# Both attentions of an audio tower: x normalised on VectorE and split into fp16 halves before the transposes

## The reference, cut to what matters

```python
h = _L0_tok_ref(x)                                   # 128 sequences of 32 tokens, 512 wide
h = h + _L0_attn_ref(_layernorm(h), wq, wk, wv, wo)  # 32 heads of 16, 8 for k and v, rotary, causal
h = h + _L0_ffn_ref(_layernorm(h), w1, w3, w2)       # ternary weights
h = h + _L1_attn_ref(_layernorm(h), Wq, Wk, Wv, Wo)  # 16 heads of 32, 4 for k and v, bias, causal
h = h + _L1_ffn_ref(_layernorm(h), gate_up, down)    # 4-bit weights
```

## Time and profile before

| | |
|---|---|
| runs | 2387.38, 2389.77, 2393.89 us |
| median | 2389.77 us |
| profiled execution | 2391.57 us |
| its span in the profile | 2389.8 us |
| mean granted clock of TensorE | 0.985 of full speed |
| busy, PE | 2244.2 us, 94% |
| busy, DVE | 1662.7 us, 70% |
| busy, ACT | 1495.3 us, 63% |
| busy, POOL | 1021.4 us, 43% |

### The profile page before, as it was taken

How to read it: one execution, slowest core, us unless ns; L and a number is a source line. 1 busy time by engine, 2 the same in 40 slices (tenths; PEclk the granted TensorE clock), 3 DMA queues, 4 the chain that set the end, 5 groups by cost and what they waited for, 6 DMA issues and landing times. The chain is left out here.

```text
span 2389.8 us, 41107 instructions
## 1 busy us (share of the span) xinstructions
PE 2244.2 (94%) x13188; PEld 1128.5 (47%) x13188; DVE 1662.7 (70%) x2931; ACT 1495.3 (63%) x2398; POOL 1021.4 (43%) x1007
## 2 busy tenths in 40 slices
PE   6999999998999996799999999999987999999998
PEld 2333333335666663344444445666652444444443
DVE  6666666665888887456667634666657888888873
ACT  4666666666788785355656425667745666667663
POOL 1222222237777773223324302444434555555552
PEclk9999999999999998799999999999999999999999
DMA  5545445442343211312223212222221011111101
GB/s 146 138 127 135 129 127 135 130 110 66 111 131 114 67 58 36 109 50 79 80 89 93 67 48 84 80 79 79 79 67 40 23 49 40 53 41 45 45 27 53
DMA packets 144300, 194.94 MB, mean 82 GB/s; under 512 B 32773, under 2 KB 76261, under 8 KB 144154
## 3 DMA queue, kind: packets, MB, share of 16 engines
q1 hardware_dynamic: 115642, 154.79, 21.7%
q10 hardware_dynamic: 28512, 38.28, 5.7%
HBM read 125.10 MB, written 42.21 MB: 70 GB/s over the span
## 5 line engine op out<-in xcount | busy, mean ns | idle before, releaser
L341 DVE TENSOR_REDUCE tm_negmax<-tm_s 128x1 f32<-128x512 f32 x512 | 323.3, 679 | 164.7 <-PE tm_s L384 164.4
L303 ACT ACTIVATE tm_prob<-tm_s 128x1024 f32<-128x1024 f32 x256 | 257.6, 1023 | 136.9 <-PE tm_s L404 130.6
L2119 PE MATMUL f_part<-f_xhi,gu 128*128 128x512 f16 x704 | 269.4, 383 | 17.8 <-ACT f_firstg L1922 6.3
L2119 PE MATMUL f_part<-f_xlo,gu 128*128 128x512 f16 x704 | 268.6, 382 | 0.0
L421 PE MATMUL tm_o<-tm_prob,tm_vt 128*64 128x512 f32 x1024 | 255.7, 620 | 0.0
L1888 POOL TENSOR_TENSOR f_firstg<-f_firstg,f_secondg 128x512 f32<-128x512 f32 x88 | 150.7, 1712 | 193.3 <-DVE f_secondg L2006 193.3
L2141 PE MATMUL f_pz<-dn,f_ghi 128*128 128x512 f16 x704 | 214.5, 380 | 5.9 <-ACT f_zc L1954 5.9
L384 PE MATMUL tm_s<-tm_qk 96*128 96x512 f16 x512 | 199.2, 391 | 14.6 <-DMA tm_qk<-tm_xs 14.1
L264 POOL TENSOR_TENSOR tm_hn<-tm_nd,tm_rows 128x1024 f32<-128x1024 f32 x32 | 75.3, 2353 | 291.8 <-DMA tm_rows<-rden 291.8
L404 PE MATMUL tm_s<-tm_qk 98*128 98x512 f16 x512 | 194.2, 382 | 1.6 <-DMA tm_qk<-tm_mrow 1.6
L975 PE MATMUL a_bankB<-a_wo,a_yThi 128*128 128x512 f16 x512 | 158.7, 393 | 4.1 <-DVE a_yTlo L899 4.0
(11 more groups left out here) (190 smaller groups left out, 5668.4 us busy)
## 6 DMA issues: line engine op xcount, KB each, us to landing
tm_qk<-tm_xs SPq DMA_DIRECT2D x384, 64.0 KB, 2.1
tm_xqk<-in_qk ACTq DMA_DIRECT2D x32, 512.0 KB, 4.3
a_hin<-h SPq DMA_DIRECT2D x64, 256.0 KB, 2.7
a_hres<-h SPq DMA_DIRECT2D x64, 256.0 KB, 3.0
h<-a_hout SPq DMA_DIRECT2D x64, 256.0 KB, 2.5
f_hin<-h SPq DMA_DIRECT2D x64, 256.0 KB, 2.7
f_hres<-h SPq DMA_DIRECT2D x64, 256.0 KB, 2.8
tm_vt<-in_vt ACTq DMA_DIRECT2D x32, 256.0 KB, 3.0
```

The costliest lines, as they stand in the source:

```text
L303: nc.scalar.activation(prob[b][:, 2 * h:2 * h + 2, :], s2[:, i % 2, :, :], ACT.Exp, scale=SCALE).then_inc(exp_done, 1)
L341: nc.vector.tensor_reduce(negmax[u][:, m:m + 1], s1[:, p % BANKS, :], AX.X, ALU.max, negate=True).then_inc(s1_read, 1)
L2119: last = nc.tensor.matmul(part[q % BANKS][:, :], (gate, up)[which][:, j, m * P:(m + 1) * P], xparts[x][u][:, j, :], start=x == 0, stop=x == 1)
```

## The change

In both attentions the normalised row is made by DVE, into one buffer (`xn` has been two). ACT casts it to the high half, and the low half is the difference, made by DVE in the first attention and by POOL in the second. Both halves lie in one buffer, `halves`, and are transposed by PE as eight fp16 blocks into bankA, which is read as 1024 fp16 columns. ACT copies both transposed halves at once into `xs` (two buffers). `offset` and the subtraction from the bank are gone. `project` reads the same operands as before from the new buffer.

```diff
-    veps, shift_by = pair("veps", [P, 1], F32), pair("shift_by", [P, 1], F32)
-    xn = pair("xn", [P, DM], F32)
-    xhi, xlo = pair("xhi", [P, KT, P], F16), pair("xlo", [P, KT, P], F16)
+    veps = pair("veps", [P, 1], F32)
+    xn, halves = sb("xn", [P, DM], F32), sb("halves", [P, 2, DM], F16)
+    xs = pair("xs", [P, 2, KT, P], F16)
...
 def gpsimd(pool):
...
+        def x_low(t):
+
+            if inside(t, TILES) and not rope:
+                wait_alone(pool, s["pool_passed"], s["high_done"], t + 1)
+                pool.tensor_tensor(halves[:, 1, :], xn[:, :], halves[:, 0, :], ALU.subtract).then_inc(s["low_done"], 1)
...
         def step(k, u):
             n = 2 * k + u
+            x_low(n + 3)
             inverse_deviation(n + 4, u)
...
 def scalar(act):
...
-        def x_hi(t, u):
+        def copy_x(t, u):
             if inside(t, TILES):
                 wait(act, s["xT_ready"], t + 1)
                 wait(act, s["kv_ready"], t - 1)
-                nc.scalar.copy(xhi[u][:, :, :], bankA[:, :].rearrange("p (j n) -> p j n", j=KT))\
-                    .then_inc(s["xhi_done"], 1)
+                nc.scalar.copy(xs[u][:, :, :, :].rearrange("p x j n -> p (x j n)"), bankA[:, :].bitcast(F16))\
+                    .then_inc(s["xs_done"], 1)
...
-        def x_normalised(t, u):
-
-            if inside(t, TILES):
-                wait(act, s["offset_done"], t + 1)
-                wait(act, s["xT_ready"], t - 1)
-                nc.scalar.activation(xn[u][:, :], hin[u][:, :], ACT.Identity, scale=rstd[u][:, :],
-                                     bias=shift_by[u][:, :]).then_inc(s["xn_done"], 1)
+        def x_high(t):
+
+            if inside(t, TILES):
+                wait(act, s["xn_done"], t + 1)
+                wait(act, s["xT_ready"], t)
+                nc.scalar.copy(halves[:, 0, :], xn[:, :]).then_inc(s["high_done"], 1)
...
-            x_hi(n + 3, 1 - u)
+            copy_x(n + 3, 1 - u)
             k_hi(n + 2, u)
-            x_normalised(n + 4, u)
+            x_high(n + 4)
...
 def vector(dve):
...
-        def offset(t, u):
+        def x_normalised(t, u):
 
             if inside(t, TILES):
                 wait(dve, s["rstd_done"], t + 1)
-                nc.vector.tensor_scalar(shift_by[u][:, :], mv[u][:, 0:1], rstd[u][:, :], -1.0,
-                                        ALU.mult, ALU.mult).then_inc(s["offset_done"], 1)
+                wait(dve, s["low_done"], t)
+                nc.vector.tensor_scalar(xn[:, :], hin[u][:, :], mv[u][:, 0:1], rstd[u][:, :], ALU.subtract, ALU.mult)\
+                    .then_inc(s["xn_done"], 1)
...
-        def x_lo(t, u):
-            if inside(t, TILES):
-                wait(dve, s["xhi_done"], t + 1)
-                nc.vector.tensor_tensor(xlo[u][:, :, :], bankA[:, :].rearrange("p (j n) -> p j n", j=KT),
-                                        xhi[u][:, :, :], ALU.subtract).then_inc(s["xlo_done"], 1)
+        def x_low(t):
+            if inside(t, TILES) and rope:
+                wait(dve, s["high_done"], t + 1)
+                nc.vector.tensor_tensor(halves[:, 1, :], xn[:, :], halves[:, 0, :], ALU.subtract)\
+                    .then_inc(s["low_done"], 1)
...
             shift(n)
+            x_low(n + 3)
             row_stats(n + 5, 1 - u, k + 2 + u)
...
             turn(n + 2, u, 1)
-            offset(n + 4, u)
             probs_lo(n)
-            x_lo(n + 3, 1 - u)
+            x_normalised(n + 4, u)
...
 def tensor(pe):
...
-                wait(pe, s["xn_done"], t + 1)
+                wait(pe, s["low_done"], t + 1)
                 wait(pe, s["yTlo_done"], t - 3)
-                for j in range(KT):
-                    last = nc.tensor.transpose(bankA[:, j * P:(j + 1) * P], xn[u][:, j * P:(j + 1) * P], ident[:, :])
+                px = bankA[:, :].bitcast(F16)
+                for x in range(2):
+                    for j in range(KT):
+                        last = nc.tensor.transpose(px[:, (x * KT + j) * P:(x * KT + j + 1) * P],
+                                                   halves[:, x, j * P:(j + 1) * P], ident16[:, :])
                 last.then_inc(s["xT_ready"], 1)
...
-                wait(pe, s["xlo_done"], t + 1)
+                wait(pe, s["xs_done"], t + 1)
...
-                wait(pe, s["xlo_done"], t + 4 if not isinstance(t, int) else min(t + 4, TILES))
+                wait(pe, s["xs_done"], t + 4 if not isinstance(t, int) else min(t + 4, TILES))
```

More of the change, by code:

```diff
@@ L511, in attention @@
     stored = [sem(f"stored{i}") for i in range(2)]
-    names = ("stats_done mv_done veps_done rstd_done offset_done xn_done xT_ready xhi_done xlo_done q_ready kv_ready "
+    names = ("stats_done mv_done veps_done rstd_done xn_done high_done low_done xT_ready xs_done q_ready kv_ready "
              "q_copied kv_copied turned_done crossed_done rot_done qhi_done qlo_done khi_done klo_done "
@@ L1013, in project @@
                 for j in range(KT):
-                    for a, w in ((xhi, wqkv[0]), (xhi, wqkv[1]), (xlo, wqkv[0])):
-                        last = nc.tensor.matmul(out, a[u][:, j, :], w[:, j, cols], start=n == 0,
+                    for x, w in ((0, wqkv[0]), (0, wqkv[1]), (1, wqkv[0])):
+                        last = nc.tensor.matmul(out, xs[u][:, x, j, :], w[:, j, cols], start=n == 0,
                                                 stop=n == 3 * KT - 1)
```

## The result

The changed kernel took 2399.53 us (median of 8 runs, 2397.5 to 2401.6), the kernel before, measured beside it, 2392.73 (8 runs, 2386.4 to 2395.7): 6.8 us more, ratio 1.0031, 95% interval 1.0019 to 1.0043. The profiled execution took 2401.11 us (span 2399.3). That is inside the range of 2388 to 2405. The forecast had +6.7 us on a median of 2389.77.

The account below looks back on a forecast made before the run. PE was taken to bound the second attention, the first being less even with ACT and DVE loaded by weight work. Terms 0.5 + 0 + 2.2 + 2.2 + 1.8 = +6.7 us on 2389.77 gave 2396.5 us, range 2388 to 2405.

Parts of the forecast that it names:

- PE's transposes: Both attentions, 64 tiles: eight fp16 transposes replace four fp32 ones on PE, 0 to 0.02 us each, taken as +0.5 us.
- Second attention: Second attention, 32 tiles: 0, because a cover of 0.5 to 0.9 us hides whichever of DVE and POOL loses the port.
- Sum tiles: First attention, 8 tiles with weight sums on ACT: late normalisation and x_high delay ACT, 8 x 0.28 = +2.2 us, bounds 0 and 4.
- What is left, 0.28, delays copy_q: Tiles with sums on ACT: 0.76 us lateness beyond ACT's idle 0.23 and 0.25 delays copy_q, then exps and PE's transposes.
- Reductions: First attention, 5 tiles with a large reduction on DVE: late y_lo delays PE's x transposes, 5 x 0.45 = +2.2 us.
- Comparisons: First attention, 8 tiles with comparisons on ACT: ACT's +0.23 us shows in full if DVE gets the port first, +1.8 us.
- rival (a): First attention: the port collides in every tile, including those with comparisons; slower, 2405 us, upper bounds +16; chance 0.17.
- Remaining tiles: First attention, tiles without load on ACT or DVE: 0, with ACT's idle time before copy_qT as the cover.
- `load`: Row loads on SP: 0, as DVE gives xn_done about when ACT did, several steps before the rows are used.
- (b): The lock costs nothing on the path, only the lower bounds show: 2392 us; chance 0.16.
- (c): Faster, 2384 us: PE no longer stands about 0.2 us before the x transposes in 30 tiles, -6; chance 0.07.
- (d): Second attention's cover too thin, POOL's wait for high_done holding inverse_deviation: +10 or more over (b), 2402 us; chance 0.05.

## Why the prediction was right, point by point

The total came out (+6.7 forecast, +6.8 measured), and the runs' ratios follow the distances: without the first column, the eight timed variants should be +0.2, +3.8, +7.5, +7.4, +12.3, +2.0, +1.6 and +1.3 us from the kernel before, and they measured -1.0, +3.8, +5.5, +6.7, +12.2, +2.9, +0.2 and +0.7, with intervals of 2 to 3.6 us to either side. But the terms did not all come out for their reasons.

- **PE's transposes, +0.5.** Measured 0. Eight fp16 transposes take 0.45 us from start to start in the first attention, as predicted. The plain tiles there are shorter by 0.02 (11.56 against 11.58), which the prediction had named as a sign against it; the second attention is longer by 0.16 in all.
- **Second attention, 0.** Right, and shown alone. The normalisation does lose to q_lo nearly every time (1.49), and the cover holds.
- **Sum tiles, +2.2.** The mechanism is right in every link of the chain, to 0.04 us in two places, though turn is only 0.19 later against cross where 0.4 to 0.6 stood, and takes 1.13 where 0.90 stood. The size is +1.32: 0.165 a tile instead of 0.28. The step that failed is "What is left, 0.28, delays copy_q": I took only ACT's two idle times as room. The distances say that another 0.1 us was absorbed; where, no row shows.
- **Reductions, +2.2.** Measured +2.40, through y_lo and PE's wait before the transposes of x, as predicted. Of it 0.6 stands in a tile (23 to 24) that I had counted among those without load.
- **Comparisons, +1.8.** Measured +2.06, but the step "ACT's +0.23 shows in full, if DVE gets the port ahead of q_lo" is wrong in both halves. DVE does not get the port: both turns at 855.38 and 857.13 are caught (0.95 and 1.35), and the normalisation at 859.54 starts 0.04 behind q_lo. x_low stands ahead of turn here, but it is not needed for this: with x_low on POOL turn is still caught in these tiles (1.14 and 1.10). The late normalisation gives 0.7 and 0.9 us in two of seven tiles, as rival (a) had it. With it out of the way 0.3 us in all is left for ACT's added time, not 1.8.
- **Remaining tiles, 0.** Right from tile 5 to 9. Wrong for 2 to 5: +1.44. In these steps POOL still has the mixer's last operations (2.37 us), and DVE's x_low took 2.14 and 1.64 us there. One took 4.55 beside the subtraction of the output weights (4.25 us) already between tiles 0 and 1, also in the profile with 21.53 for the first column, where it cost nothing. I priced x_low by plain tiles alone and did not look at what else POOL runs in the first steps. That these collisions are the cost is not shown: with x_low earlier and the longest of them gone (0.68 for 2.14) the distance stayed.
- **`load`, 0.** Right for the changed kernel, where DVE does not wait for a row from 600 us to the end of the first attention. The reason, that the rows come several steps before they are used, is wrong: the load waits for the normalisation of one step and its row is read in the next, and in the run with x_low on POOL DVE waited 0.33 us for it.
- **Rivals.** (a), a collision in nearly every tile (22 of 25), is what the trace shows; its price of +16 did not come, since most collisions are hidden. (b) and (c) did not occur. Of (d), POOL does wait for x_high three times at the start of the second attention (7.9 us in all, the longest 5.8), but the distances there grew by 0.16 us together. The chances don't quite add up as written: a third of the forecast with (a) and (d) is 0.40 for slower, not 0.38.

So the total was right partly by luck, by errors that cancelled: 0.9 too much in the sums and 0.5 too much on PE, against 1.4 too little in the first tiles and 0.2 to 0.3 in the reductions, the comparisons and the second attention each.

The lock itself: the Trainium skill ("SBUF — State Buffer", Who interferes with whom) also says that a VectorE instruction with two operands in SBUF contends with a GpSimd instruction that reads SBUF. The trace agrees: x_low, with two operands in SBUF, took 4.55 us beside POOL's 4.25. y_lo and pTlo, with one operand in PSUM, keep their durations all through both attentions (0.68 or 0.69 for y_lo; 1.21 to 1.23 for pTlo in the first, 0.69 at half the width in the second).

## What to carry to other kernels

When an instruction that shares a port with another engine is moved, price the position and not only the length: here 0.6 us of work ahead of turn moved three later instructions behind POOL's, and the cost appeared 5 us later on a third engine. Look for the collisions in the first and last steps of a stage too, where the other stage's long operations run. And before a term is put down to an engine's added work, see whether the collision can be taken away with the work left in place: with the order changed from tile 6 on, distances 5 to 31 were those of before with the same 0.23 us still on ACT.

## What was not expected of the hardware

- With starts 0.05 us apart, the record's order doesn't tell who had the port. In the second attention the normalisation starts at 1608.55 and q_lo at 1608.60, yet q_lo takes its usual 1.16 us and the normalisation 1.49, ending 0.28 after q_lo as in the earlier trace rows.
- A caught instruction ends behind POOL's by a time of its own, whatever POOL's length. In the changed kernel it was 0.14 us for the second turn of 128 columns (704.10 against 703.96), 0.28 for the normalisation of 512 (706.55 against 706.27), and 0.54 and 0.55 for x_low of 512, behind operations of 2.37 and 4.25 us. So the cost of a collision can be read from when POOL ends.
- A DVE normalisation that reads and writes even and then odd elements takes 0.54 to 0.59 us, as the one over neighbours does.
- One program on one core had its first two tiles at 24.02 us in one execution and at 21.53 in another, by the level of PE's clock after stretches in which PE was mostly idle. Another had 33.93 and 35.51 us over the next three tiles in the same way. Two single profiles that differ by as much in such a place say nothing about the change.
